# Layer 1 of a four-layer kernel laid out as one line of 80 units instead of four chunks between barriers

## The reference

```
xn = layernorm(x)
# s: a recurrence over the tokens (wkv)
shifted = xn moved by one token
k, v, r = (xn*mix + shifted*(1-mix)) @ Wk, Wv, Wr ; r = sigmoid(r)
per token:  max_out = max(mx, k+tf); e1 = exp(mx-max_out); e2 = exp(k+tf-max_out)
            out = (e1*num + e2*v) / (e1*den + e2)
            max_st = max(mx+td, k); num, den carried with exp(mx+td-max_st), exp(k-max_st)
s = (r * out) @ Wo
# f: mixture of experts, 8 routed (top 2 of the router's logits, softmax) and 2 shared
for e in 10 experts: f += weight_e * (silu(xn @ w1.T) * (xn @ w3.T)) @ w2.T      # 128 -> 256 -> 128
x = x + s * silu(f)
```

## Time and profile before

| | us |
|---|---|
| median of 3 runs (3302.0 to 3304.8) | 3302.27 |
| profiled execution, its own time | 3312.2 |
| span of the profile | 3310.0 |
| PE busy | 3108.1 (94%) |
| DVE busy | 2423.0 (73%) |
| ACT busy | 1744.0 (53%) |
| POOL busy | 851.6 (26%) |
| mean granted clock of PE | 0.962 |

### The profile page before, as it was taken

The page is one execution under the profiler, slowest core; times in us unless marked ns, Lnnn a source line. Parts: engine busy times, 40 slices in busy tenths (PEclk is TensorE's granted clock), DMA queues, the critical chain, the costliest instruction groups (busy, mean ns, idle before and its releaser), DMA issues. The chain is left out here.

```text
span 3310.0 us, 57446 instructions
## 1 busy us (share of the span) xinstructions
PE 3108.1 (94%) x20342; PEld 2429.1 (73%) x20342; DVE 2423.0 (73%) x5195; ACT 1744.0 (53%) x3960; POOL 851.6 (26%) x706
## 2 busy tenths in 40 slices
PE   5999998979889799999689999999999999999998
PEld 4777675546455577778577888888888888888887
DVE  4878774755656445556677888888888888888888
ACT  2445543332314244443475666666666666666666
POOL 2101100100101200000343344444444444444443
PEclk9989998989899889989899999999999999999999
DMA  2000101000000000000300011000000110000000
GB/s 53 2 4 34 44 26 48 1 1 1 1 1 1 0 1 1 1 1 1 78 1 3 20 22 22 22 11 20 16 20 22 22 22 9 22 14 22 22 1 26
DMA packets 43551, 53.04 MB, mean 16 GB/s; under 512 B 8645, under 2 KB 27272, under 8 KB 43272
## 3 DMA queue, kind: packets, MB, share of 16 engines
q1 hardware_dynamic: 39298, 47.02, 5.7%
q10 hardware_dynamic: 3974, 2.37, 0.3%
HBM read 38.63 MB, written 10.75 MB: 15 GB/s over the span
## 5 line engine op out<-in xcount | busy, mean ns | idle before, releaser
L75 PE MATMUL banks<-scratch 128*128 128x128 f32 (+3 forms) x3648 | 715.4, 325 | 11.5 <-ACT scratch L2671 8.9
L75 PE MATMUL banks<-nT,w 128*128 128x512 f32 x1184 | 573.9, 606 | 22.3 <-issue 13.6
L75 PEld LDWEIGHTS banks<-scratch 128*128 128x128 f32 x3648 | 482.8, 192 | 77.0 <-issue 59.8
L75 PEld LDWEIGHTS banks<-scratch,tb 128*128 128x128 f32 x2560 | 356.5, 191 | 101.9 <-issue 61.5
L75 PE MATMUL banks<-scratch,tb 128*128 128x128 f32 x2560 | 368.5, 275 | 0.0
L3114 POOL TENSOR_TENSOR scratch<-scratch,aT 128x1024 f32<-128x1024 f32 x128 | 358.8, 2803 | 4.5 <-DVE aT L2936 4.5
L83 DVE SCALAR_TENSOR_TENSOR scratch<-scratch,tb 128x512 f32<-128x512 f32 (+3 forms) x512 | 339.7, 705 | 8.4
L75 PEld LDWEIGHTS banks<-nT,w 128*128 128x128 f32 x1184 | 204.5, 194 | 173.6 <-issue 150.0
L83 DVE SCALAR_TENSOR_TENSOR scratch<-tb,nn,banks 128x512 f32<-128x512 f32 (+3 forms) x512 | 267.7, 543 | 75.7 <-PE banks L75 71.6
L3106 POOL TENSOR_TENSOR scratch<-backwards,nn 128x512 f32<-128x512 f32 x128 | 133.0, 1039 | 736.3 <-ACT nn L3026 736.3
L2936 DVE TENSOR_TENSOR aT<-banks,turn 64x1024 f32<-64x1024 f32 x256 | 312.9, 1222 | 5.7
(11 more groups left out here) (396 smaller groups left out, 5307.0 us busy)
## 6 DMA issues: line engine op xcount, KB each, us to landing
tb<-head_rows SPq DMA_DIRECT2D x32, 512.0 KB, 7.0
turn<-head_turns SPq DMA_DIRECT2D x64, 128.0 KB, 2.7
head_turns<-loads SPq DMA_DIRECT2D x16, 256.0 KB, 2.8
head_turns<-rotation SPq DMA_DIRECT2D x16, 256.0 KB, 2.9
xs<-in_x SPq DMA_DIRECT2D x8, 256.0 KB
w<-in_L_Wqk SPq DMA_DIRECT2D x16, 128.0 KB, 2.0
out<-xs SPq DMA_DIRECT2D x8, 256.0 KB, 2.3
w<-in_L_w1T SPq DMA_DIRECT2D x1, 1280.0 KB, 9.3
```

The source lines that it names most:

```text
L75: return self.T.matmul(out, lhsT, rhs, start=start, stop=stop, skip_group_check=True)
```

## The change

Layer 1 becomes one line of 80 units. A unit v is one expert for one sequence of one chunk: v = 20c + 2e + b. `l1_slots` goes over slots s from -35 to 85 and gives for each s a function `due(d)` with the chunks c for which 20c + d = s. Each engine has its own list of what a slot holds, so a unit's work stands in different slots on different engines: `up(s - 1)` and `outputs(s - 3)` on PE, `silu(s + 5, 1)`, `silu(s + 6, 0)` and `weighted(s + 3)` on ACT, `hidden(s + 3, 1)`, `hidden(s + 4, 0)` and `accumulate(s)` on DVE. The openings, projections, recurrence, routing and closings of a chunk stand in slots of other chunks' units. There is one barrier, after the layer.

Banks: 0 and 1 for half 0 (w1, w3), 2 and 3 for half 1, 4 + b for outputs of sequence b, 6 + b in turn for openings, projections, logits (6) and Wo. Each turn waits for the one before to be emptied. `nT1`, `cw`, and the sum of the experts are there twice (by c % 2).

ACT now multiplies the outputs of a routed expert by their weights (`weighted`: four activations of 128 x 128 with a scale operand; for the shared experts one of 128 x 512), and DVE only adds 128 x 512. The gate is made with Silu instead of Tanh and two passes, the half that Tanh needs for receptance goes into Wo (`rwo`, once, made under layer 0), and closings are made by sequence: Silu, product with bank 6 + b, add. Layer 3 takes over eight semaphores of layers 1 and 2 instead of new ones. The diff, cut:

```diff
@@ ahead work under layer 0
+        k.made_step(k.ts(k.rwo[:, :], k.rwo[:, :], 0.5))
@@ layer 1
+    UNITS1 = 20 * CHUNKS
+    def l1_slots(self):
+        for s in range(-35, 86):
+            yield s, lambda d: [c for c in range(CHUNKS) if 20 * c + d == s]
+    def l1_pe(self):
...
+        def up(v, m):
+            c, e, b = k.l1_unit(v)
+            x = k.nT1[c % 2][:, b, 1:1 + S]
+            k.l1_emptied_of(T, b, "open", c, b)
+            if v == 0:
+                T.wait_ge(k.l1_weights.sem, 48)
+            k.after(T, k.l1_hid[m], v)
+            k.mm(k.bank(2 * m), k.w1[:, e, m * P:(m + 1) * P], x)
+            k.mm(k.bank(2 * m + 1), k.w3[:, e, m * P:(m + 1) * P], x).then_inc(*k.l1_up[m].up())
+        def outputs(v):
+            c, e, b = k.l1_unit(v)
+            for m in range(2):
+                k.after(T, k.l1_hid[m], v + 1)
+            k.after(T, k.l1_yo, v - 1)
...
+        for s, due in k.l1_slots():
+            for c in due(0):
+                project(1, c, 0)
+            for c in due(24):
+                mixed(c, 1)
+            for c in due(-1):
+                project(0, c, 0)
+            if 0 <= s - 1 < k.UNITS1:
+                up(s - 1, 0)
+            if 0 <= s - 3 < k.UNITS1:
+                outputs(s - 3)
+            for c in due(1):
+                logits(c)
+            for c in due(2):
+                project(1, c, 1)
+            for c in due(11):
+                project(2, c, 0)
+                project(2, c, 1)
+            for c in due(-4):
+                open_turn(c, 0)
+                open_turn(c, 1)
+            if 0 <= s - 1 < k.UNITS1:
+                up(s - 1, 1)
+            for c in due(23):
+                mixed(c, 0)
+            for c in due(-1):
+                project(0, c, 1)
+    def l1_dve(self):
...
+        for s, due in k.l1_slots():
...
+            if 0 <= s + 3 < k.UNITS1:
+                hidden(s + 3, 1)
...
+            if 0 <= s + 4 < k.UNITS1:
+                hidden(s + 4, 0)
...
+            if 0 <= s < k.UNITS1:
+                accumulate(s)
...
+    def l1_act(self):
...
+        def weighted(v):
+            c, e, b = k.l1_unit(v)
+            to, y = k.yo1[v % 2], k.bank(4 + b).rearrange("p (t d) -> p t d", d=D)
+            k.after(A, k.l1_y, v + 1)
+            k.after(A, k.l1_acc, v - 1)
+            if e < 8:
+                k.after(A, k.l1_cw, c + 1)
+                for t in range(TPB):
+                    x = A.activation(to[:, t, :], y[:, t, :], ACT.Identity,
+                                     scale=k.cw[c % 2][:, b * TPB + t, e:e + 1])
...
+        for s, due in k.l1_slots():
...
+            if 0 <= s + 5 < k.UNITS1:
+                silu(s + 5, 1)
...
+            if 0 <= s + 6 < k.UNITS1:
+                silu(s + 6, 0)
...
+            if 0 <= s + 3 < k.UNITS1:
+                weighted(s + 3)
...
+    def l1_pool(self):
...
@@ layer 3
-        k.m3_filled = {b: Count(nc, f"m3_filled{b}") for b in (0, 1, 2, 4, 6, 7)}
+        k.m3_filled = {b: n.again() for b, n in zip((0, 1, 2, 4), k.l1_filled + k.l2_filled)}
...
@@ run
-                        for c in range(CHUNKS):
-                            k.layer1(c)
+                        k.layer1()
```

More of the change, by code:

```diff
@@ L119, in constants @@
         k.normed = k.sb("normed", [P, NT, D])
[L120 to L148, removed]
@@ L152, in open_layer @@
[L152 to L181, removed]
+        k.moments, k.rstds, k.scaled, k.gated = (
+            Count(k.nc, n) for n in ("moments", "rstds", "scaled", "gated"))
@@ L1356, in l1_project_act @@
[L1356 to L1366, removed]
@@ L1381, in first_largest @@
             k.step(V.tensor_tensor(out, q, col(2), ALU.is_equal))
[L1383 to L1390, removed]
@@ new lines, in before, with maxima, decay @@
+        def before(c, n):
+            k.after(V, k.l1_mixV, 16 * c + n)
+        def maxima(c, b):
+            k.l1_emptied_of(V, b, 0, c, b)
+            V.tensor_tensor_scan(mx[:, b, cols], k.td[:, 0:1].broadcast_to([D, S]), kT[:, b, cols],
+                                 -1e38, ALU.add, ALU.max).then_inc(*k.l1_mixV.up())
+        def decay(c):
+            before(c, 2)
+            for b in range(B):
+                k.l1_filled_by(V, b, "mixed", c - 1, b)
+            k.stt(F1, mp, k.td[:, 0:1], mn, ALU.add, ALU.subtract).then_inc(*k.l1_mixV.up())
@@ new lines, in carried, with with_new, reciprocal @@
+        def carried(c, over):
+            k.after(V, k.l1_mixA, 4 * c + 4)
+            k.after(V, k.l1_mixG, 4 * c + 4)
+            before(c, 9)
+            V.tensor_tensor(MO if over else F1, E1, (den if over else num)[:, :, prev], ALU.mult).then_inc(*k.l1_mixV.up())
+        def with_new(c, over):
+            before(c, 12 if over else 10)
+            to = MO if over else F1
+            V.tensor_tensor(to, to, E2 if over else F2, ALU.add).then_inc(*k.l1_mixV.up())
+        def reciprocal(c):
+            before(c, 13)
+            V.reciprocal(MO, MO).then_inc(*k.l1_mixV.up())
@@ new lines, in quotient, with received, close_product @@
+        def quotient(c):
+            before(c, 14)
+            V.tensor_tensor(F1, F1, MO, ALU.mult).then_inc(*k.l1_mixV.up())
+        def received(c):
+            before(c, 15)
+            for b in range(B):
+                k.l1_emptied_of(V, b, 2, c, b)
+            k.stt(F1, R, 1.0, F1, ALU.add, ALU.mult).then_inc(*k.l1_mixV.up())
+        def close_product(c, b):
+            t = k.normed[:, b * TPB:(b + 1) * TPB, :]
+            k.l1_filled_by(V, b, "mixed", c, b)
+            k.after(V, k.gated, 2 * c + b + 1)
+            V.tensor_tensor(t, t, k.bank(6 + b).rearrange("p (t d) -> p t d", d=D), ALU.mult).then_inc(
+                *k.l1_emptied[b].up())
@@ new lines, in out_value @@
+        def out_value(c):
+            done()
+            k.after(G, k.l1_mixA, 4 * c + 3)
+            G.tensor_tensor(F2, E2, Vv, ALU.mult).then_inc(*k.l1_mixG.up())
+        for s, due in k.l1_slots():
+            for c in due(4):
+                key_weight(c)
+            for c in due(7):
+                key_value(c)
+            for c in due(-33):
+                open_power(c, 0)
+                open_power(c, 1)
+            for c in due(16):
+                carried(c)
+            for c in due(17):
+                out_value(c)
@@ L1583, in layer2_prepare, with layer1 @@
+    def layer1(self):
+        k = self
+        k.l1_pe()
+        k.l1_dve()
+        k.l1_act()
+        k.l1_pool()
+        k.meet()
     def layer2_prepare(self):
```

496 lines of the change are left out of this document (300 added, 196 removed).

## The result

The changed kernel takes 3225.88 us (median of four runs, 3218.13 to 3229.45) against 3303.14 us beside it: ratio 0.9763, 95% interval 0.9742 to 0.9783, or 2.4% faster. The prediction was 3223.0 us.

The account below looks back on a forecast made before the run. PE bounds the kernel, idle or at half clock between chunks' expert stages. First expert matmul at 561.2, plus 470.2 of work, 12 of stalls and 4.7 of end: 1048.1 instead of 1126.76, gain 79, 3223 us; 8-in-10 range 3209 to 3254.

Parts of the forecast that it names:

- Start: Layer 1's opening: first expert matmul at 561.2 against 571.63, 10.4 us gained, bound by the w2 load.
- The unit: One expert for one sequence on PE: two ups of 1.72 us and outputs of 1.79, together 5.22 us.
- Middle: PE work from the first expert matmul to outputs(79): 470.2 us without stalls, ending at 1031.4.
- can't place: Expert stage before took 109.9 us where pitches, cold start and stalls explain 109.0; 0.9 a chunk carried, 3.6 in all.
- Stalls: PE waiting for late ACT or DVE: exponentials 0.8 us a chunk, last reciprocal 2.4; 9.2 with the unexplained, taken as 12.
- rival 3: Turns of banks 6 and 7 stand away from their data, so the kernel is slower, 3338 if half a slot late; chance 0.03.
- Other engines: Layer 1: ACT busy 268 us with 40 table loads, DVE about even, POOL 44, the layer's four DMAs unchanged.
- End: From outputs(79) to layer 2's moments: 4.7 us, with the last Wo hidden beside it.
- Layers 2 and 3: They start from the same state, PE cold and barrier passed, and keep their times.
- Rival 1: PE's clock or thin idle everywhere in the line: at clock 0.93, 33 us go, gain 46, 3256 us; chance 0.12.
- Rival 2: Every exponential's burst on ACT stalls PE in full: 69.6 us in all, gain 13, 3289 us; chance 0.06.
- Rival 4: Better than counted: no stall and nothing of the unexplained, 12 us less, 3211 us; chance 0.12.

Follow-up runs that it names:

- The four lines: Changed kernel with each chunk's 20 units as a line alone, a barrier after each chunk or only after the last: 3257.57 and 3252.44 us, layer 1 536.7 and 533.6 us.

## Why the prediction was right

- **What bounds the kernel.** The mechanism held: the gain is 57.8 us of PE's waits and 21.1 of its half clock. The four lines show its two parts, 43.8 us inside the chunks and 37.8 between them.
- **Start.** Forecast 14.9 us from the layer's start to the first expert matmul, bound by w2; measured 14.8, with PE's last wait for w2.
- **The unit.** Forecast 5.22 us. PE's timeline in the steady line shows it from one unit's outputs to the next but for the projections:

```profile
856.19 1.95 PE L75 MATMUL banks<-w,hidden 128*128 128x128 f32 x16
857.97 1.02 PE L75 MATMUL banks<-nT,rw_now 128*128 128x512 f32 x2
...
861.41 3.60 PE L75 MATMUL banks<-nT,w 128*128 128x512 f32 x8
864.84 1.95 PE L75 MATMUL banks<-w,hidden 128*128 128x128 f32 x16
```

  Sixteen records of outputs take 1.78 (857.97 - 856.19), eight of up 3.43 (864.84 - 861.41): 5.21.
- **Middle.** Forecast 470.2 of work and 12 of stalls, 482.2 us; measured 479.4 (558.70 to 1038.10). The 9.2 beyond the sum are 3.5 of waits for hidden, 3.4 of two falls of the clock, and 2.3 spread thinly, which no experiment placed. The terms of the forecast add up to the same 9.2, and that is luck: the waits for hidden were forecast at 5.6 and came to 3.5, and the 3.6 that I "can't place" came to 5.7, of which 3.4 are now placed, at the logits. The 2.8 that I put on top, for 12, weren't needed.
- **Stalls.** The second exponential in a row: 0.8 forecast, 0.34 measured. Last reciprocal: 2.4 and 2.10. The other reciprocals, carried, gap, routing and the turns: nothing, as forecast. That settles rival 3: PE never waits for a turn between 558 and 1039.
- **Other engines.** ACT 259.7 us busy, forecast 268, with 41 table loads, forecast 40. DVE came out 32 us lower, not "about even": 301.4 against 333.3. The multiply-adds that went weighed more than the adds that came, and one instruction of the recurrence got faster (below). It was worth nothing either way.
- **End.** Forecast 4.7 us from outputs(79) to layer 2's moments; measured 4.68.
- **Layers 2 and 3.** "Keep their times" was 4.6 us off: 2183.2 before, 2178.6 after, and layer 1 started 2.4 us earlier. Neither is to be put down to the change: over the thirteen profiles of the changed kernel and its variants, which share the other layers, layer 1's start lies anywhere from 534.95 to 549.53, and layers 2 and 3 take 2174.3 to 2189.3. This is why the span fell by 88.6 us and the layer by 81.6.
- **The whole.** The median fell by 77.3 us, forecast 79.3. The changed kernel's own three medians lie between 3222.0 and 3225.9, so a miss of 2.9 us says nothing more about the terms than the layer in the trace does.

Rival 1 (the clock) was real in kind, and it is what the prediction's sum did not have: its first reason against a fall was that the experts run at 1.00, but two falls stand right behind the logits, inside the line, which the prediction had named as a sign of being wrong. They cost 3.4 us instead of the 33 that the rival needed. Rival 2 falls with the line's own waits (of the five bursts a chunk one stalls PE, 0.34 us) and with the kernel that gave ACT 150 us more. Rival 4, a line without stalls, is refuted by the 9.2 us. Of the Trainium skill's price for a switch of tables ("ScalarE: Activation LUTs", "What ACT_TABLE_LOAD costs") only the load of 1.28 us is there again; the Silu starts 0.02 us after it (723.77 + 1.28, 725.07), so there is no room for the drain of 1.38.

## What to carry to other kernels

Between stages that all engines enter together, PE pays twice: for the wait, and for the 1.2 GHz level after it. One line of units that holds the neighbours' openings and closings in its slots removes both, and its length can be had from pitches within 1%. Count slack by the slot, not by the engine's busy share: ACT at 82% cost this line nothing more, since no added burst passed the slot's slack, while DVE's one 6.5 us instruction was seen at 60%.

## What the runs showed of the hardware

- PE's granted clock can fall while PE is busy without a gap, right behind 2.2 us of the logits' small matmuls: 16 of 28 times, 1.70 us each. With the logits in two halves with 3.6 us of other matmuls between, it didn't in chunks 1 to 3 (0 of 9, against 11 of 21); with 4.3 us in a row it fell each time. PE's busy row shows no dip there; the granted clock and the lengths of the records give it away. The Trainium skill ("TensorE: Matmul & The Clock Gate", "What's actually happening") says that the gate follows how busy PE has been. The traces count PE as busy all through, so the profile's busy time didn't foretell these falls.
- Three DVE instructions of this kernel are longer beside a POOL product of 128x1024. The timeline in the routing of chunk 1, after:

```profile
695.09 2.01 POOL L1748 TENSOR_TENSOR scratch<-scratch 128x1024 f32<-128x1024 f32 x1 [59.39 <-DVE scratch L1497]
695.26 1.92 DVE L1484 TENSOR_TENSOR route<-route,route_top 128x64 f32<-128x64 f32 x1
```

  That 128x64 product takes 0.225 us in the kernel before and 1.91 in all four chunks now. The other way round, the instruction of 128x1024 with td takes 2.66 us in the kernel before, where POOL's product runs beside it, and 1.28 now, alone. The 128x64 product ends as if it had run only once POOL was nearly done (POOL 695.09 + 2.01 = 697.10, DVE 695.26 + 1.92 = 697.18). The third is the add of the experts' outputs (L1433, 128x512): 1.90 us in the four places where POOL's last product of the recurrence runs, 0.69 elsewhere. The Trainium skill ("GPSIMD Engine Reference", "Specifications") says that the two engines contend for SBUF where a DVE instruction has two SBUF inputs, and all three have. The trace agrees on the other side too: `hidden` (L1424), which reads one of its inputs from a PSUM bank, takes 0.69 us beside the same product. No experiment parted the two engines; the pairing is what the timelines show.
- The same work ahead of layer 1 takes 535 to 550 us from one execution to the next, with mean clocks of 0.969 to 0.978 over the span. For a change of a few us, the layer in the trace tells more than the time.
